# Cross-attention kernel on one core: the image part of unit 13 by matrix products, and the image exponentials one slot later

## What is computed

```python
text_out = softmax(q @ k_t.T * scale) @ v_t            # 252 text tokens
qsem = l2norm(probs_t @ text_ehs)                      # norm of the text part, per head and row
sem  = qsem @ l2norm(ip_ehs).T
probs_ip = softmax(q @ k_ip.T * scale + 0.5 * sem) * spatial_mask   # 4 image tokens
out = (text_out + probs_ip @ v_ip) @ W_out + b_out + residual
```

## Time and profile before

| | us |
|---|---|
| median of three runs (817.98 to 822.62) | 821.95 |
| the profiled execution | 818.06 |
| its span on the core | 816.3 |
| PE busy in the span | 780.0 (96%) |
| DVE / ACT / POOL busy | 562.7 / 425.4 / 402.3 |
| mean granted clock of TensorE | 0.985 of full |

### The profile page before, as it was taken

How to read it: one execution, slowest core, us unless ns; L and a number is a source line. 1 busy time by engine, 2 the same in 40 slices (tenths; PEclk the granted TensorE clock), 3 DMA queues, 4 the chain that set the end, 5 groups by cost and what they waited for, 6 DMA issues and landing times.

```text
span 816.3 us, 17251 instructions
## 1 busy us (share of the span) xinstructions
PE 780.0 (96%) x6392; PEld 634.3 (78%) x6392; DVE 562.7 (69%) x1539; ACT 425.4 (52%) x911; POOL 402.3 (49%) x297
## 2 busy tenths in 40 slices
PE   5979999999999999999999999999999999988796
PEld 5977778788888878787877788787887888766574
DVE  5447445757575767667858778788697797687745
ACT  5234624554546474647465465565555655555551
POOL 6421202201202040403658976887779768779763
PEclk9989989999999999999999999999999999999999
DMA  8874632946546564636353345254172342400010
GB/s 275 220 208 139 185 110 66 240 127 175 143 132 175 177 160 114 166 112 164 108 121 113 94 113 163 63 120 149 35 186 83 87 120 65 137 1 16 21 33 17
DMA packets 103027, 100.67 MB, mean 123 GB/s; under 512 B 10264, under 2 KB 102176, under 8 KB 102944
## 3 DMA queue, kind: packets, MB, share of 16 engines
q1 hardware_dynamic: 101408, 98.26, 43.7%
q10 hardware_dynamic: 1536, 1.31, 0.5%
HBM read 61.65 MB, written 36.74 MB: 121 GB/s over the span
## 4 chain that ended last, share of the span: by engine, by line
PE 75%; DVE 7%; issue 4%; SPq 4%; DMA 3%; ACT 3%; POOL 3%; POOLq 0%; DVEq 0%; ACTq 0%
PE pB L379 21%; PE pB L495 13%; PE pB L458 8%; PE pB L481 7%; PE pB L579 5%; PE pPV L522 4%; PE pPV L517 4%; PE pPV L527 4%; PE pB L536 3%; PE pPV L513 2%; POOL Y L1280 2%; DVE m_sb L1041 2%; DMA KP<-k0d 1%; DMA q1d<-qlo 1%; ACT P L842 1%
## 5 line engine op out<-in xcount | busy, mean ns | idle before, releaser
L1280 POOL TENSOR_TENSOR Y<-P,wv 128x512 f32<-128x512 f32 x120 | 156.3, 1319 | 109.2 <-ACT P L842 109.0
L1056 DVE TENSOR_TENSOR Y<-pB,Y 128x512 f32<-128x512 f32 x160 | 108.8, 685 | 68.9 <-PE pB L495 59.2
L458 PE MATMUL pB<-KP,QP 96*128 96x256 f32 x640 | 130.5, 289 | 4.5 <-DMA KP<-k0d 2.1
L458 PEld LDWEIGHTS pB<-KP,QP 96*128 96x128 f32 x640 | 107.1, 192 | 18.7 <-issue 7.3
L1257 POOL TENSOR_TENSOR klo<-xin,khi 128x256 fp32r<-128x256 f32 x18 | 13.2, 757 | 215.2 <-ACT khi L753 215.2
L1041 DVE TENSOR_REDUCE m_sb<-pB 128x2 f32<-128x504 f32 x160 | 107.9, 675 | 11.5 <-PE pB L458 9.8
L481 PE MATMUL pB<-QP,KP 100*128 100x512 f32 x320 | 109.4, 422 | 3.2 <-DMA QP<-mlo 2.7
L842 ACT ACTIVATE P<-pB 128x512 f32<-128x512 f32 x160 | 86.5, 596 | 44.8 <-PE pB L481 34.9
L842 ACT ACTIVATE P<-pB,ln 128x512 f32<-128x512 f32 x160 | 101.3, 692 | 0.0
L832 ACT ACTIVATE wv<-pB 128x512 fp32r<-128x512 f32 x120 | 66.8, 591 | 55.2 <-PE pB L481 53.9
L753 ACT ACTIVATE Vs<-pPV 128x512 f32<-128x512 f32 (+1 forms) x80 | 39.4, 492 | 100.8 <-PE pPV L517 67.5
(11 more groups left out here) (176 smaller groups left out, 1714.3 us busy)
## 6 DMA issues: line engine op xcount, KB each, us to landing
QP<-q0d SPq DMA_DIRECT2D x64, 192.0 KB, 4.1
KP<-k0d SPq DMA_DIRECT2D x64, 192.0 KB, 4.3
c_sb<-in_cT SPq DMA_DIRECT2D x16, 512.0 KB, 5.1
q0d<-qhi SPq DMA_DIRECT2D x32, 256.0 KB, 2.5
k0d<-khi SPq DMA_DIRECT2D x30, 256.0 KB, 2.5
q0d<-qlo SPq DMA_DIRECT2D x16, 256.0 KB, 2.8
k0d<-klo SPq DMA_DIRECT2D x15, 256.0 KB, 2.8
VB<-vipd SPq DMA_DIRECT2D x6, 640.0 KB, 4.0
```

The source lines that it names most:

```text
L458: made = mm(bank[:, sc * S:sc * S + S], QP[i][0:KROWS, j, a, sc * 128:sc * 128 + 128], KP[i][0:KROWS, j, :], start=True, stop=True)
L1056: tt(Y[:, p, dst, :], bank_of["gp", q, dst][:, :], Y[:, p, dst, :], MUL).then_inc(dv_y, 1)
L1280: tt(Y[:, p, ch, :], P[:, p, ch, :], PH[q % HR][ch].bitcast(F32), SUB).then_inc(po_y, 1)
```

## The change

`UF` = U - 3 = 13 takes the place of U - 2 wherever the closing units are told from the mixed ones. Units 8 to 12 are mixed; 13, 14 and 15 are closing. GpSimd's mixing steps, the load of the image values and VectorE's add are done for five units in place of six, and unit 13's end moves to the slots of the closing form. Second, ScalarE runs the image exponentials at `shares` (slot 2) and no more at `soft` (slot 1), for all units; in slot 2 they stand behind the text exponentials of that slot. The last unit's end, written out behind the loop, is as before.

```diff
+UF = U - 3
@@
-    return B <= u < U - 2
+    return B <= u < UF
@@
-    return u - (U - 2) + 1
+    return u - UF + 1
@@ def output(u, part):
-                if u == U - 2:
+                if u >= UF:
                     pe.wait_ge(ac_wt, closing_no(u))
                     pe.wait_ge(ac_mb, closing_no(u))
@@
-                        made = mm(bank[0:M, n * S:n * S + S], l, r, start=(k == 0), stop=(k == len(pairs) - 1 and u != U - 2))
-                    if u == U - 2:
+                        made = mm(bank[0:M, n * S:n * S + S], l, r, start=(k == 0), stop=(k == len(pairs) - 1 and u < UF))
+                    if u >= UF:
                         made = mm(bank[0:M, n * S:n * S + S], Mb[:, m * 128:m * 128 + M], wT[:, :], start=False, stop=True)
@@ scalar_program, image_weights_back and image_values
-                ac.wait_ge(po_mix, U - 2 - B)
+                ac.wait_ge(po_mix, UF - B)
@@ scalar_program, the walk through the plan
-                        elif what == "soft":
+                        elif what == "soft" and not (True):
+                            image_weights(*a)
+                        elif what == "shares" and True:
                             image_weights(*a)
@@ vector_program, image_shares
-                dv.wait_ge(po_mix, min(k, U - 2 - B))
-                if u == U - 1:
+                dv.wait_ge(po_mix, min(k, UF - B))
+                if u > UF:
                     dv.wait_ge(pe_wt, closing_no(u - 1))
@@ vector_program, image_values
-                dv.wait_ge(po_mix, U - 2 - B)
-                if u == U - 2:
+                dv.wait_ge(po_mix, UF - B)
+                if u == UF:
                     then(nc.vector.memset(bdh[64:128, 2, :, :].bitcast(F32), 0.0))
```

## The result

The change makes the kernel slower. Over 5 runs its median is 831.81 us (828.86 to 834.71) against 819.3 for the kernel before in the same comparison; the ratio is 1.0141, with a 95% interval of 1.0118 to 1.0164. The forecast was -1.0 us and the range ended at 825.0, so both are missed. The profiled execution took 828.86 us, span 827.1, against 816.3.

A forecast was written before the change was run, and what follows sets the result against it. TensorE was taken as the bound, full in turns 10 to 13, with room only in turns 14 and 15. Turn 15's +1.5, -1.0, -0.95 and -0.55 gave -1.0 us: 821.95 to 820.9 us, range 815.5 to 825.0.

The forecast's parts named there:

- Part 1: Image exponentials a slot later: 0 in turns 9 to 13, 0 in turn 14, a gain only in turn 15.
- a term of between 0 and -1.1: Turn 15: the 40-column product, 1.31 us there and 0.20 in the tail, gets shorter; middle value -0.55 us taken.
- its -1.0 and -0.95: Turn 15: VectorE's wait before the normalisation goes, -1.0 us; TensorE's second half of value products starts earlier, -0.95 us.
- Part 2: Unit 13 closed by products instead of mixing, in turn 14: shift 2.95 us later, TensorE 1.4 us ahead at turn's end.
- w at 723.64 as before: Turn 14: VectorE, running without a gap, finishes unit 13's shares w at 723.64, unchanged.
- The shift 2.95 us later: Turn 14: with the closing work ahead of it, the shift falls at 743.05 instead of 740.10.
- 9.1 us from the shift to the last slot's scores: Turn 14: this stretch falls from 13.45 to 9.1 us without the stall, transposes and output parts, ending at 752.15.
- Square roots 1.5 us later: End of turn 14: GpSimd's square roots for heads 0 to 15 begin at 752.1 instead of 750.61.
- Part 3: Turn 15: softmax ends 1.5 us later, then savings of 1.0, 0.95 and 0.55 us; sum -1.0 us.
- (b): Rival: new TensorE waits in turns 14 and 15 halve its clock, about 1.6 us each; +2.2, 824.1 us; chance 0.22.
- (a): Rival: all idle time in turns 14 and 15 turns into gain, ceiling 9.3 us, half 4.6: 817.3 us; chance 0.18.
- (c): Rival: nothing nets, since the 1.5 us of later square roots eats both savings; 0, 822.0 us; chance 0.12.

The follow-up runs named there:

- e4: The changed kernel with unit 8's image exponentials back in slot 1, all other units as in the change; 827.33 us, ratio 1.0072 to the kernel before.
- e5: The kernel before plus filler on GpSimd behind its slot-1 differences: two-operand products in turns 9 to 11, fills in 12 and 13; 825.11 us, one run.
- e1: The kernel before with only the later image exponentials, the last two units closing as before; 826.58 us, ratio 1.0064.
- e2: The kernel before with only unit 13 closed by products, image exponentials in slot 1 as before; 823.72 us, ratio 1.0043.
- e8: e2 plus idle TensorE products in turns 14 and 15, put into banks just taken, where TensorE would stand; 822.65 us, ratio 1.0034 to the kernel before.
- e3: The changed kernel plus one wait holding GpSimd's slot-2 differences until VectorE's softmax is done; 821.63 us, ratio 1.0017 to the kernel before.
- e6: The changed kernel with e3's hold, unit 8's exponentials in slot 1, and unit 13's first transposes of O in slot 3; 820.38 us, ratio 0.9991.
- e9: e6 plus 6 and 6 idle TensorE products into the banks of unit 13's transposes of O and w; 818.81 us, ratio 0.9985 to the kernel before.
- e7: The kernel before with late image exponentials and the hold on GpSimd's slot-2 differences in turn 15 only; 819.65 us, ratio 0.9991.
- e12: The changed kernel plus 16, 6 and 14 idle TensorE products where TensorE stands in turns 14 and 15; 830.30 us, ratio 1.0121 to the kernel before.

## Why the prediction was wrong

**What bounds the kernel.** Right as far as it went. But it read "TensorE is busy 54.9 of 55 us" off turns 11 and 12 and applied it to turns 9 to 13. Turn 9, with W_out's split in it, is no such turn: 2.68 us there (e4), half of them by the gap and half by the clock behind it. The prediction itself named a change in the length of turns 9 to 13 as a sign of being wrong. And e5 shows that even turns 10 and 11 lengthen by 1.3 us once VectorE is held for 1.9.

**Part 1, the later exponentials, "worth 0 here".** This is the step that failed. It noted that ScalarE's stall keeps GpSimd waiting, counted on the stall's end to bring Y 3 us earlier, and never asked what GpSimd would then run beside. It did see 1.31 against 0.20 us for one product and called it GpSimd's work, but only as a term of between 0 and -1.1, with no end on the other side. Measured, the order is a loss of 5.3 us where the prediction had a gain in turn 15 (its -1.0 and -0.95) and 0 elsewhere. Turn 9 lost 2.7 to 4.2 us, turn 14 had +1.9 us in the softmax and +0.8 at the shares; in turn 15:

```profile
771.63 1.38 DVE L1098 TENSOR_TENSOR t<-ST,rn 128x160 f32<-128x160 f32 x1 [0.55 <-POOL rn L1306]
773.04 1.28 DVE L1100 TENSOR_TENSOR t<-t,invip 128x160 f32<-128x160 f32 x1
774.36 1.31 DVE L1102 TENSOR_TENSOR t<-t,ipS 128x160 f32<-128x160 f32 x1
...
779.69 1.27 DVE L1121 TENSOR_TENSOR w<-ex,rm 128x160 f32<-128x160 f32 x1
```

The square roots of that turn end at 759.26 + 5.43 = 764.69, and the softmax begins at 771.63, 6.94 us later; before it was 6.99. From there to VectorE's next Y product (776.92; before 766.76) it took 5.3 us in place of 3.7. The sum of the order's part is 5.3 us (e1; 3.0 to 7.5 by its interval), 7.9 by the stages of e1's one trace, one of them in the tail. With the closing's 3.5 (e2; 1.6 to 5.5) that makes 8.8 of the 11.6 us by which the changed kernel is slower; whether the other 2.8 are the two working together or the spread of the runs is not shown.

**Part 2, the closing.** "w at 723.64 as before": confirmed by e2 (33.73 against 33.71 us behind the shift), and refuted in the changed kernel only through Part 1. "The shift 2.95 us later": 6.0 in e2, of which 2.05 go when the clock is kept up (e8), leaving 4.0: the mechanism was right, the size short by 1, what is left of it not traced further. By whole times the closing costs 3.5 us. "9.1 us from the shift to the last slot's scores": 8.7 (750.44 to 759.16). "Square roots 1.5 us later", that is 9.0 behind the shift: 8.8, at 759.26. "The row DMAs hold": nothing waited for them.

**Part 3, turn 15.** Predicted from the shift to the tail's softmax: 66.09 - 1.47 of square roots - 2.5 = 62.1. With GpSimd held the kernel does it in 61.75, 61.64 and 61.68 (e3, e6, e9). That it comes so near is in part luck. In e3 the stretch from the softmax to w is 2.1 us shorter than before where the sum had 1.55, since the 40-column product took 0.20 us and not the middle value; behind w it is 0.5 shorter and not 0.95, since the clock did not stay up (0.50 from 769 to 773). In the changed kernel it took 65.46, by the slow products and by TensorE's waits:

```profile
771.13 1.93 PE L528 MATMUL pPV<-Y,y 128*32 128x256 f32 x16 [1.61 <-DVE Y L1059]
...
781.11 0.62 PE L562 MATMUL pB<-ident,w 128*80 128x128 f32 x2 [2.27 <-DVE w L1121]
```

TensorE stands 1.61 us for the Y product that VectorE brings late, and 2.27 us before the transposes of w, which end the turn's wait for VectorE. The product at 774.36 alone is 1.0 us over its 0.33, and so is w's at 779.69. Some 1.3 us more went with the clock behind the second gap, as e4 shows.

**The rivals.** (b) was a real effect and had the better claim than its 0.22: both waits came (1.01 us before the third maximum, 2.35 with the hold, and 2.27 before w's transposes), and it was priced at 1.6 us a time where 2.05 and 1.6 were measured in turn 14 and about 1.3 in turns 9 and 15. It did not decide the sign; at +2.2 it would have stayed inside the range. The true cause was not among the rivals: that a wait which goes may have been another engine's quiet. (a) and (c) fell. That a gap of about 2.5 us halves the clock is also not a rule: e7 had the same gap as the kernel before, in the same place, and kept its clock there, while it fell behind the shift, after a second gap of 2.60 us. A gap of 2.60 in the same place in e1 left the clock at 1.00 (748 to 756).

```profile
722.04 0.44 PE L537 MATMUL pB<-ident,Vs 128*128 128x128 f32 x2 [2.53 <-ACT P L843]
```

```profile
722.00:724.00 2.00, 1.82 (x8) 1.37 (x9) 1.93 (x9) 1.42 (x3) 1.93 (x2) 1.00 0.00 0
...
742.00:744.00 2.00, 2.00 (x6) 1.51 (x6) 1.30 (x1) 1.92 (x5) 2.00 (x3) 0.50 0.04 9
```

**The chances.** 0.09 for slower by over 0.5% was far too low; the sum was made of gains with losses bounded at zero, which is how the range came to end at 825.

## What to carry to other kernels

An idle engine may be doing others a service: before freeing a stalled engine, list what it and those fed by it will then run beside, and look in the trace for instructions of one shape with two durations, such as 0.33 and 1.3 us, since the slow ones tell which pair collides. If a reorder loses, try it again with the collision held off by one wait: here that turned the loss in turn 9 into a gain, and with the edit kept to turns 9 and 15, and filler on TensorE, it beat the kernel before by 0.5%. And where TensorE waits just ahead of a stretch that it paces, filling the gap with useless products gave back 2.05 and 1.6 us of a turn; where a short fall of the clock lay beside another engine's work it gave nothing. Last, if a stage contains such a gap, its length can differ by 1.3 us or so between two executions of one code, so look at the granted clock before putting a difference down to an edit.

## What the runs showed of the hardware

A VectorE product with two SBUF operands waited not for one GpSimd instruction but for three back to back: 3.36 us in place of 0.33, until GpSimd ran out of work at 446.5. That was no accident of one execution: e1 and e12 have 3.36 and 3.37 in the same place. In turn 14 each of three products got its turn after one instruction (1.3 us). What decides between the two isn't settled by these runs. GpSimd's fills had no effect at all, and GpSimd paid little: its differences took 1.26 to 1.37 us a piece beside the waiting VectorE, against some 1.27 alone, and its part of W_out's split 1.64 and 0.96 us against 1.55 and 0.86. The granted clock behind TensorE's gaps of about 2.2 to 2.6 us differed between executions of the same code: 0.79, 0.59 and 0.57 in turn 9, 0.51 and 1.00 in turn 14.
